# One product with ones for each unit instead of two, and a new place for it, in a clustered 1x1 convolution

## The reference, cut to what matters

```python
xn = x / max(norm(x, over channels), 1e-12);  cn = centroids / max(norm(centroids), 1e-12)
sim = einsum('bchw,nc->bnhw', xn, cn)
idx = argmax(sim, over n);  onehot = one_hot(idx, 40)
centroids_local = einsum('bhwn,bchw->bnc', onehot, x) / max(count, 1)
gathered = centroids_local[b, idx]
delta = gathered - x                              # per position, 512 channels
alpha = exp(-mean(delta * delta, over channels))  # one number for each position
y = x + alpha * delta
out = relu(einsum('oc,bchw->bohw', W, y) + b)
```

## Time and profile before

| | us |
|---|---|
| median of three runs | 431.25 (431.1 to 432.02) |
| the profiled execution | 431.4 |
| its span | 429.6 |
| PE busy | 422.2 |
| DVE busy | 285.3 |
| ACT busy | 243.4 |
| POOL busy | 206.7 |

### The profile page before, as it was taken

How to read it: one execution, slowest core, us unless ns; L and a number is a source line. 1 busy time by engine, 2 the same in 40 slices (tenths; PEclk the granted TensorE clock), 3 DMA queues, 4 the chain that set the end, 5 groups by cost and what they waited for, 6 DMA issues and landing times.

```text
span 429.6 us, 5789 instructions
## 1 busy us (share of the span) xinstructions
PE 422.2 (98%) x2134; PEld 296.0 (69%) x2134; DVE 285.3 (66%) x378; ACT 243.4 (57%) x329; POOL 206.7 (48%) x102
## 2 busy tenths in 40 slices
PE   8999999999999999999999999999999999999996
PEld 6744466775777667775867757776677758777785
DVE  2368979485776767495883857767674956787730
ACT  5665385566465673565754664656735657555541
POOL 2000665486284482674553862844826745424330
PEclk9999999999999999999999999999999999999999
DMA  8996298976577946859379665879463220222123
GB/s 275 309 291 122 56 261 219 274 218 166 143 244 185 226 168 164 215 149 256 99 198 265 169 175 142 242 182 229 163 170 125 98 99 0 98 99 98 49 112 134
DMA packets 70927, 73.94 MB, mean 172 GB/s; under 512 B 2724, under 2 KB 45732, under 8 KB 70900
## 3 DMA queue, kind: packets, MB, share of 16 engines
q1 hardware_dynamic: 70900, 73.58, 61.9%
HBM read 48.40 MB, written 25.17 MB: 171 GB/s over the span
## 4 chain that ended last, share of the span: by engine, by line
PE 95%; DVE 2%; ACT 1%; issue 1%; POOL 0%; POOLq 0%; DVEq 0%
PE main L797 20%; PE main L799 20%; PE main L798 20%; PE sump L740 10%; PE fa L700 9%; PE gat L771 5%; PE al L778 1%; PE fa L709 1%; PE al L779 1%; PE al L819 1%; PE fa L724 1%; PE main L840 1%; PE al L785 1%; PE gat L785 1%; PE gat L812 1%
## 5 line engine op out<-in xcount | busy, mean ns | idle before, releaser
L284 POOL TENSOR_TENSOR z<-z,x 128x1024 f32<-128x1024 f32 x42 | 99.3, 2384 | 147.1 <-DVE z L389 147.1
L797 PE MATMUL main<-yh,wh 128*128 128x512 f32 x376 | 152.5, 406 | 0.0
L799 PE MATMUL main<-yh,wl 128*128 128x512 f32 x376 | 147.0, 391 | 0.0
L798 PE MATMUL main<-yl,wh 128*128 128x512 f32 x376 | 146.7, 390 | 0.0
L291 POOL TENSOR_TENSOR yl<-z,yh 128x1024 fp32r<-128x1024 f32 x44 | 106.0, 2423 | 57.9 <-ACT yh L530 57.9
L369 DVE TENSOR_TENSOR z<-gat,x 128x1024 f32<-128x1024 f32 x46 | 56.2, 1221 | 91.1 <-PE gat L771 91.1
L538 ACT ACTIVATE o<-main,bcol 128x512 f32<-128x512 f32 x96 | 65.7, 686 | 82.8 <-PE main L799 82.8
L797 PEld LDWEIGHTS main<-yh,wh 128*128 128x128 f32 x376 | 70.7, 188 | 20.4 <-issue 4.6
L799 PEld LDWEIGHTS main<-yh,wl 128*128 128x128 f32 x376 | 70.6, 188 | 15.2
L798 PEld LDWEIGHTS main<-yl,wh 128*128 128x128 f32 x376 | 70.7, 188 | 14.3
L530 ACT ACTIVATE yh<-z 128x1024 fp32r<-128x1024 f32 x48 | 50.5, 1052 | 22.9 <-POOL z L284 21.9
(11 more groups left out here) (114 smaller groups left out, 325.5 us busy)
## 6 DMA issues: line engine op xcount, KB each, us to landing
x<-x SPq DMA_DIRECT2D x24, 1024.0 KB, 5.7
out<-o SPq DMA_DIRECT2D x23, 1024.0 KB, 4.8
xs<-x SPq DMA_DIRECT2D x84, 256.0 KB, 6.3
o<-w SPq DMA_DIRECT2D x1, 1024.0 KB, 12.3
out<-o SPq DMA_DIRECT2D x4, 256.0 KB, 2.1
sq<-centroids SPq DMA_DIRECT2D x2, 80.0 KB
bcol<-bias SPq DMA_DIRECT2D x1, 2.0 KB, 11.7
```

The lines of the kernel that those rows point to most:

```text
L284: pool.tensor_tensor(z, z, X[g // PARTS % 2][:, pair(h), span(g)], ALU.add).then_inc(y_pool, 1)
L797: t_.matmul(main[:, o % 2, :], WH[:, k, rows], YH[g % 2][:, k, :], start=(k == 0), stop=False)
L798: t_.matmul(main[:, o % 2, :], WH[:, k, rows], YL[g % 2][:, k, :], start=False, stop=False)
L799: last = t_.matmul(main[:, o % 2, :], WL[:, k, rows], YH[g % 2][:, k, :], start=False, stop=(k == KC - 1))
```

## The change

- SH and SL, 128x512 each, become one 128x512 tile SHL, whose partitions 0 to 63 take the high part and 64 to 127 the low part. Before the split the upper 64 partitions of al are added to the lower 64: `move_upper` (ACT) copies al[64:128] to partitions 0 to 63 of a tile in SBUF, `fold` (DVE) adds that to al[0:64]. `high_sum` and `low_sum` then work on 64 partitions, and `sum_squares` is one matmul.
- `sum_squares(g)` stands behind the fourth convolution group in every iteration; that of unit 2, which stood ahead of the loop, stands in iteration 3 behind convolve(1,0).
- `exp(g)` on ACT moves to the next iteration, behind relu(g-2,3).
- On DVE parts_of_mean(1) comes before low_sum(2). With p == 1 the first step of the argmax (`best_sims`) comes before `low_sum`, the others (`first_best`) behind it, and the second transpose_half behind these.
- On ACT high_half(g-1,1) comes before high_sum(g), `means` is split with `move_upper` between its parts, and relu(g-2,0) goes ahead of both where p == 2.
- keep_busy(9) becomes keep_busy(6).

```diff
+LOW = P // 2
-        SH = sb("sh", [P, UNIT], F32R)
-        SL = sb("sl", [P, UNIT], F32R)
+        upper_sum = sb("upper_sum", [LOW, UNIT], F32)
+        SHL = sb("shl", [P, UNIT], F32R)
...  DVE
+            def fold(g):
+                dve.wait_ge(upper_done, folded(g))
+                v_.tensor_tensor(al[0:LOW, :], upper_sum[:, :], al[0:LOW, :], ALU.add).then_inc(fold_done, 1)
             def low_sum(g):
                 dve.wait_ge(sh_done, folded(g))
-                wait(dve, one_done, g)
-                v_.tensor_tensor(SL[:, :], al[:, :], SH[:, :].bitcast(F32), ALU.subtract).then_inc(sl_done, 1)
+                v_.tensor_tensor(SHL[LOW:P, :], al[0:LOW, :], SHL[0:LOW, :].bitcast(F32), ALU.subtract
+                                 ).then_inc(sl_done, 1)
...
             add_squares(2)
             rest_of_mean(1)
+            parts_of_mean(1)
+            fold(2)
             low_sum(2)
-            parts_of_mean(1)
             transpose_half(6, 0)
             transpose_half(6, 1)
...
                 add_squares(g)
-                if beside and p < 2:
+                if beside and p == 0:
                     transpose_half(g + 4, 1)
+                fold(g)
                 if beside and p == 2:
                     rest_of_mean(b + 1)
+                if beside and p == 1:
+                    best_sims(b + 1)
                 low_half(g - 1, 1)
                 low_sum(g)
                 if beside and p == 1:
-                    argmax(b + 1)
+                    first_best(b + 1)
+                    transpose_half(g + 4, 1)
...  ACT
+            def move_upper(g):
+                act.wait_ge(s_done, folded(g))
+                a_.activation(upper_sum[:, :], al[LOW:P, :], ACT.Copy).then_inc(upper_done, 1)
             def high_sum(g):
-                act.wait_ge(s_done, folded(g))
+                act.wait_ge(fold_done, folded(g))
                 wait(act, one_done, g)
-                a_.activation(SH[:, :], al[:, :], ACT.Copy).then_inc(sh_done, 1)
+                a_.activation(SHL[0:LOW, :], al[0:LOW, :], ACT.Copy).then_inc(sh_done, 1)
...
             square(2, 1)
-            means(1)
+            scale_means(1)
+            high_means(1)
+            move_upper(2)
             high_half(1, 1)
             high_sum(2)
             relu(0, 2)
-            relu(0, 3)
-            exp(2)
             for g in range(PARTS, UNITS):
+                relu(g - 3, 3)
                 if g > PARTS:
-                    relu(g - 3, 3)
+                    exp(g - 1)
                 square(g, 0)
                 if beside and p == 2:
                     high_half(g - 1, 0)
...
                     high_half(g - 1, 1)
-                    means(b + 1)
                     relu(g - 2, 0)
+                    scale_means(b + 1)
+                    move_upper(g)
+                    high_means(b + 1)
                     high_sum(g)
                     relu(g - 2, 1)
                 else:
                     relu(g - 2, 0)
+                    if g == PARTS:
+                        exp(g - 1)
                     square(g, 1)
...
                     if not beside:
                         relu(g - 2, 1)
+                    move_upper(g)
+                    high_half(g - 1, 1)
                     high_sum(g)
-                    high_half(g - 1, 1)
                     if beside:
                         relu(g - 2, 1)
                 relu(g - 2, 2)
-                exp(g)
...  PE
-                t_.matmul(al[:, :], ones[:, :], SH[:, :], start=True, stop=False)
-                t_.matmul(al[:, :], ones[:, :], SL[:, :], start=False, stop=True).then_inc(one_done, 1)
+                t_.matmul(al[:, :], ones[:, :], SHL[:, :], start=True, stop=True).then_inc(one_done, 1)
...
-            keep_busy(9)
+            keep_busy(6)
...
             convolve(0, 3)
-            sum_squares(2)
...
                     convolve(g - LAG, 0)
+                    if g == PARTS:
+                        sum_squares(g - 1)
                     gather(g, 1)
...
                 convolve(g - LAG, 2)
-                if beside:
-                    sum_squares(g)
                 convolve(g - LAG, 3)
-                if not beside:
-                    sum_squares(g)
+                sum_squares(g)
```

More of the change, by code:

```diff
@@ L153, in build @@
         pair_done, s_done, sh_done, sl_done = sem("pair_done"), sem("s_done"), sem("sh_done"), sem("sl_done")
+        upper_done, fold_done = sem("upper_done"), sem("fold_done")
         one_done, exp_done, za_done = sem("one_done"), sem("exp_done"), sem("za_done")
@@ L317, in transpose_half, with best_sims @@
                     last.then_inc(tr_done, 1)
-            def argmax(b):
-                shape = [P, PARTS * TILES, N]
+            def best_sims(b):
                 dve.wait_ge(simT_done, b + 1)
@@ L323, in argmax, with first_best @@
                 v_.tensor_reduce(best[:, :], simT, AXIS_X, ALU.max).then_inc(arg_step, 1)
+            def first_best(b):
+                shape = [P, PARTS * TILES, N]
                 dve.wait_ge(arg_step, 4 * b + 1)
@@ L431, in _ @@
             keep_transposed()
-            argmax(0)
+            best_sims(0)
+            first_best(0)
             for k in range(KC):
@@ L444, in _ @@
                 delta(g, 1)
-            argmax(1)
+            best_sims(1)
+            first_best(1)
             scale(0, 0)
@@ L567, in copy_sums, with scale_means @@
                 a_.activation(sumsH[:, :], sumP[:, :], ACT.Copy).then_inc(sumsH_done, 1)
-            def means(b):
+            def scale_means(b):
                 act.wait_ge(rc_step, 2 * b + 2)
@@ L572, in means, with high_means @@
                 a_.activation(mean(b), mean(b), ACT.Copy, scale=rcount[:, :]).then_inc(mean_step, 1)
+            def high_means(b):
                 act.wait_ge(mean_step, 2 * b + 1)
@@ L607, in _ @@
             evacuate_onehot(0)
-            means(0)
+            scale_means(0)
+            high_means(0)
             act.wait_ge(b_in, 16)
@@ L670, in _ @@
             relu(g - 2, 3)
+            exp(g)
             relu(g - 1, 0)
```

## The result

The changed kernel takes 429.94 us (median of 7 runs, 429.57 to 430.51) against 431.86 for the kernel before on the same chip (7 runs, 431.1 to 432.27). The ratio is 0.9958, 95% interval 0.9946 to 0.9969: faster by 0.4%. The forecast was 429.8 (427.8 to 431.5). The span of the profiled execution fell from 429.6 to 427.9 us.

What follows compares the result with a forecast made beforehand. PE was taken to bound the kernel. Terms: -0.4 (start) + 3.2 (to gather(4,0)) - 4.6 (units 4 to 23) + 0.3 (last three) = -1.5 us, giving 429.8 against the median, range 427.8 to 431.5.

Steps and rivals of the forecast that it cites:

- The bound: PE, busy 422.2 of 429.6 us, bounds the kernel; a wait laid on it costs its full length wherever it falls.
- step 1: Units 2 to 23: one matmul fewer each, 22 x 0.23 = 5.1 us off PE if nothing else makes it wait.
- The cost of move_upper and fold (2): Each unit: two more instructions, taken as 0.59 us on ACT and 0.68 on DVE; both engines have the time.
- rival C: move_upper and fold take longer than their rows; slower from 0.3 us more each, 435.2 at double; chance 0.08.
- Unit 2 (3): Unit 2 and image 1's means: convolve(1,0) waits for relu(0,2) behind fold and high_sum(2), 1.1 us.
- Iteration 3 (4): convolve(1,3) waits 1.9 us for relu(1,1) behind high_sum(3), the largest term; gather(4,0) 3.2 us late.
- Iterations 4 to 20 (5): The later place of sum_squares covers the longer chain at no cost; tightest at p = 1, 0.8 us left.
- rival D: Iterations with p = 1 lack the margin; 0.25 us of PE wait in each of six gives 431.3; chance 0.07.
- The last three units (6): PE waits for low_sum, which loses its 0.09 us overlap with low_half by writing other partitions: 3 x 0.09 = 0.3 us.
- keep_busy (7): At the start: six passes fewer let the first similarities begin earlier, gain bounded by 0 and 0.45, taken as 0.4 us.
- Rival B: At the start: fewer passes leave a hole, PE's clock rises late, costing 1.5 us, so 431.3; chance 0.10.
- Rival A: The order at unit 2 costs little, one or both early waits missing: 426.3 to 427.9 us; chance 0.18.

Runs made afterwards that it cites:

- The second run: The changed kernel with relu(0,2) put ahead of high_sum(2) on ACT: 429.86 us, ratio 0.9965 to the kernel before.
- the kernel whose profile has a wait of 2.0 us: The changed kernel with sum_squares(g) put back behind the third convolution group in iterations 3 to 20: 431.05 us, ratio 0.9986.
- the start repaired: The changed kernel with relu(1,1), relu(0,2), relu(1,0), exp(2) moved earlier and transposes of units 6 and 7 reordered: 428.57 us, ratio 0.993.
- the one with two moves: The changed kernel with a second copy of al[64:128], to an unused tile, ahead of move_upper: 432.78 us, ratio 1.0037.

## Why the prediction was right, point by point

*The bound.* Right in that PE is the engine to count on: it is busy for 97% still. Too strong is that a wait laid on PE costs its full length wherever it falls: the wait of 1.18 us before convolve(1,0), taken away, gave nothing, as PE then waited 1.7 us for DVE's delta(3,0) instead of 0.5. The sum was not hurt by it, since it follows the lists up to gather(4,0) and doesn't add up waits.

*One matmul fewer (step 1).* Right, and a little low. 0.23 was forecast; doubling the product gave 0.23 to 0.24 over the whole kernel and 0.245 in iterations 4 to 20, and these iterations gained 0.25 each.

*The cost of move_upper and fold (2).* Right, at the durations taken. The three lines, each 22 times, ns min/median/max:

```profile
L535 ACT ACTIVATE upper_sum<-al x22: 594/596/599, 62.6 to 398.8; 64x512 f32<-64x512 f32 x22
...
L387 DVE TENSOR_TENSOR al<-upper_sum,al x22: 657/689/689, 64.7 to 399.4; 64x512 f32<-64x512 f32 x22
...
L391 DVE TENSOR_TENSOR shl<-al,shl x22: 683/685/689, 66.0 to 401.6; 64x512 fp32r<-64x512 f32 x22
```

On 64 partitions they take as long as their rows on 128, so rival C fell.

*Unit 2 (3).* The wait is there, 1.18, where 1.1 was forecast for the delay of convolve(1,0). Its chain is the one given: fold, high_sum, relu(0,2). The second run showed that it alone is worth nothing, which the step implied by letting gather(3,1) be set by DVE, though it did not say so.

*Iteration 3 (4).* Right, 1.76 idle for 1.9, with relu(1,1) behind high_sum(3) as its cause (shown by moving it). gather(4,0) came at 85.05, forecast 85.24 less 0.4 for the start: 0.2 more than forecast.

*Iterations 4 to 20 (5).* Right: no PE wait. With p = 1, relu(g-2,1) is done 0.72 us before it is needed, forecast 0.8:

```profile
194.22 0.67 ACT L557 ACTIVATE o<-main,bcol 128x512 f32<-128x512 f32 x1
195.61 0.39 PE L824 MATMUL main<-yh,wh 128*128 128x512 f32 x1
```

So rival D fell.

*The last three units (6).* Right, with its small term. They gained 0.12 each for 0.23 - 0.09 = 0.14. low_sum no longer overlaps low_half, which ends at 389.09:

```profile
387.86 1.23 DVE L412 TENSOR_TENSOR yl<-z,yh 128x1024 fp32r<-128x1024 f32 x1 [0.26 <-ACT yh L549]
389.12 0.69 DVE L391 TENSOR_TENSOR shl<-al,shl 64x512 fp32r<-64x512 f32 x1
```

It starts 0.03 behind it, where it began 0.09 before its end. That the place of its output is the cause, and not its 64 partitions, is shown by the run with two products of 64 rows: there it writes 64 partitions from 0 on, and the overlap of 0.09 is back. The Trainium skill's rule in "VectorE: DVE Perf Modes", section "Two Vector instructions with no wait between them", forecasts this, and the trace agrees, here and at unit 2, where the transpose behind low_sum starts 0.04 behind its end (65.99 + 0.68 = 66.67 and 66.71).

*keep_busy (7).* Right in the profile (33.75 to 33.35), 0.3 between medians. Rival B did not occur in the profile of the kernel after: the similarities' weight loads are at 137 ns. In six of the other ten profiled kernels with six matmuls it occurred in part, 0.1 to 0.5 us of the 1.5. With three matmuls it occurred in full, at 2.25 us in the profiled execution.

*Rival A.* Its heading has 426.3 to 427.9, but its own sum gives 426.1 for the lower end. Its upper case, only the first wait left, is what the run with relu(1,1) moved measured: 427.74.

*The sum.* -1.5 forecast; the profiled executions give -1.7, the medians of the same session -1.9, the ratio's interval -2.3 to -1.3. Two small errors work against each other: gather(4,0) came 0.2 later than forecast, and iterations 4 to 20 gained 4.3 us instead of 3.9. And it is luck that the time itself is within 0.1 of 429.8, as the kernel before had a median of 431.25 in three runs when I forecast and 431.86 in seven.

## What to carry to other kernels

Where one engine bounds the kernel, a saving repeated in every iteration is easy to read; what decides the result are the single places where the new order queues something the bound engine needs behind something slow: here 5 us saved in 22 units, 3.4 given back in three waits at unit 2 and in iteration 3, and 4.7 more won by moving a relu, some transposes and a subtraction. Before repairing a wait, ask what the waiting engine needs next: the 1.2 us before convolve(1,0) were worth nothing until DVE's list was shortened too. And when a step that frees a buffer is moved, follow the loads queued behind its semaphore: that cost 2.1 us in one run.

## What the runs showed of the hardware that I had not expected

- Two fp32r products with 64 rows of weights, between matmuls with 128, cost 0.98 us up to the gather; the two with 128 rows cost 0.70 counted in the same way (99.75 to 100.45, one step of 0.23 ahead of the rows shown). The first load of 64 rows did not overlap the matmul ahead, and all three steps were longer, 0.32 to 0.34.
- Where the output of a DVE instruction starts decides whether it overlaps the one ahead: with 64 partitions from 0 on low_sum began 0.09 us before the end of low_half, with 64 to 127 it began 0.03 behind it. The copy by ACT from partitions 64 to 127 to 0 to 63 took 0.596 us, no longer than the copy of 128 partitions in the kernel before, 0.600.
- Behind one wait of 2.23 us, in a kernel otherwise dense on PE, the granted clock was 1.2 GHz for 3.4 us, which cost 1.6 us more. A wait of 1.76 us in the profile of the kernel after did not, and its seven runs lie within 1 us at a mean granted clock of 0.999 to 1.0. Of the kernel whose profile has a wait of 2.0 us, six of twelve executions had a mean of 0.996 and were 2.1 us longer. One execution each of the runs with relu(0,2) moved (432.21), with the product twice (436.98) and with the start repaired (429.59) had 0.996 too; the profiles of these kernels are of other executions, with waits of 1.8, 1.8 and 2.1 us and a clock of 1.00 through them. So one execution of a kernel can show the lower clock and the next not; only the one with two moves was profiled with it.
